# A new slot table for the stages of a chunked delta-rule attention kernel

## What is computed

```
q, k, v = silu(short_conv(x @ W))          # 4 taps along time, 56 tiles of 128 channels
beta = 2 sigmoid(x @ Wb);  g = -exp(A_log) softplus(x @ Wa + dt_bias)
q, k = l2norm(q) / sqrt(d), l2norm(k)
def step(S, t):                            # scan over 1024 tokens, S is 128x128 per head
    S = S * exp(g[t])
    for i in range(3):
        S = S + beta[i] * outer(k[i], v[i] - k[i] @ S)
    return S, q @ S
o = o * rsqrt(mean(o*o) + 1e-5) * rms_weight * silu(x @ Wg)
x = layernorm(x + o @ Wo)
x = layernorm(x + moe(x))
```

## Time and profile before

| | |
|---|---|
| runs | 8394.54, 8353.07, 8391.29 us |
| profiled execution | 8395.38 us, span 8393.3 us |
| granted clock of TensorE, mean | 0.938 |
| TensorE: matmuls, weight loads | 7601.8 us (91%), 6484.1 us (77%) |
| VectorE | 6505.2 us (78%) |
| ScalarE | 5331.5 us (64%) |
| GpSimd | 4114.8 us (49%) |
| moved by DMA | 97.66 MB, 12 GB/s |

### The profile page before, as it was taken

How to read it: one execution, slowest core, us unless ns; L and a number is a source line. 1 busy time by engine, 2 the same in 40 slices (tenths; PEclk the granted TensorE clock), 3 DMA queues, 4 the chain that set the end, 5 groups by cost and what they waited for, 6 DMA issues and landing times. The chain is left out here.

```text
span 8393.3 us, 425998 instructions
## 1 busy us (share of the span) xinstructions
PE 7601.8 (91%) x155940; PEld 6484.1 (77%) x155940; DVE 6505.2 (78%) x22297; ACT 5331.5 (64%) x19575; POOL 4114.8 (49%) x6333
## 2 busy tenths in 40 slices
PE   4799999999999999999999999999999999979999
PEld 1688888888888888888888888888888888857777
DVE  3888888888888888888888888888888888623333
ACT  2666677766766666767666666766776676523333
POOL 0355555555555555555555555555555555511111
PEclk6799999999999999999999999999999999989999
DMA  2000000000000000000000000000000000010000
GB/s 87 6 10 9 10 10 10 10 9 9 10 9 10 9 10 9 10 9 9 10 9 10 9 9 10 9 9 9 10 10 9 9 10 9 8 31 8 10 7 8
DMA packets 283622, 97.66 MB, mean 12 GB/s; under 512 B 226096, under 2 KB 276544, under 8 KB 281152
## 3 DMA queue, kind: packets, MB, share of 16 engines
q1 hardware_dynamic: 281408, 68.93, 3.8%
HBM read 52.08 MB, written 16.78 MB: 8 GB/s over the span
## 5 line engine op out<-in xcount | busy, mean ns | idle before, releaser
L802 DVE SCALAR_TENSOR_TENSOR CY<-PP,CWV,CY 128x128 f32<-128x128 f32 x4608 | 1585.2, 344 | 102.4 <-ACT CY L721 18.0
L802 DVE SCALAR_TENSOR_TENSOR CY<-PP,CWK,CY 128x128 f32<-128x128 f32 x4608 | 1581.9, 343 | 97.6 <-ACT CY L721 26.9
L1014 POOL TENSOR_TENSOR UM<-U,C 32x256 f32<-32x256 f32 x1536 | 1104.7, 719 | 120.2 <-POOL UM L1014 23.1
L1007 POOL TENSOR_TENSOR Y<-U,C 32x256 f32<-32x256 f32 x768 | 554.0, 721 | 1224.1 <-DVE UQ L895 1183.9
L536 PE MATMUL PI<-T,WB 32*32 32x32 f32 x49152 | 750.2, 196 | 302.1 <-DVE T L811 297.3
L536 PEld LDWEIGHTS PI<-T,WB 32*32 32x32 f32 x49152 | 638.4, 110 | 466.8 <-issue 402.4
L516 PE MATMUL PP<-XT,WV 128*128 128x131 f32 x3072 | 741.5, 324 | 157.8 <-DVE CY L802 99.3
L516 PE MATMUL PP<-XT,WK 128*128 128x131 f32 x3072 | 783.5, 340 | 85.0 <-DVE CY L802 84.8
L721 ACT ACTIVATE CY<-PP,CWK 128x128 f32<-128x128 f32 x1536 | 563.1, 367 | 397.9 <-PE PP L516 387.6
L987 POOL TENSOR_TENSOR S<-R,BETA 96x4 f32<-96x4 f32 x512 | 101.3, 198 | 1421.7 <-DVE R L855 1421.7
L791 ACT ACTIVATE KQ<-CY 128x128 f32<-128x128 f32 x2048 | 738.7, 361 | 7.9
(11 more groups left out here) (228 smaller groups left out, 19287.5 us busy)
## 6 DMA issues: line engine op xcount, KB each, us to landing
EX<-exd SPq DMA_DIRECT2D x768, 32.0 KB, 2.2
exd<-EXS SPq DMA_DIRECT2D x16, 512.0 KB, 2.7
XR<-in_L_attn_x SPq DMA_DIRECT2D x65, 64.0 KB, 2.7
XL<-in_L_attn_x SPq DMA_DIRECT2D x16, 256.0 KB, 2.8
XRES<-in_L_attn_x SPq DMA_DIRECT2D x64, 64.0 KB, 2.7
x<-X SPq DMA_DIRECT2D x64, 64.0 KB, 1.6
XI<-x SPq DMA_DIRECT2D x16, 256.0 KB, 2.8
out<-OUT SPq DMA_DIRECT2D x16, 256.0 KB, 2.3
```

Source lines behind the costliest of these rows:

```text
L802: dve.scalar_tensor_tensor(CY[:, m % RING], ptile(m)[:, s:s + P], taps_of(m)[:, s:s + 1], CY[:, m % RING], ALU.mult, ALU.add).then_inc(tap ...
L1007: pool.tensor_tensor(Y1[r, :, :], U[r, par, :, r], over(first[r, :], [BK, NHEAD, BK], 1), ALU.mult).then_inc(seed_sb, 1)
L1014: pool.tensor_tensor(UM[r, lv], U[r, par, :, r], over(merge[lv][r, :], [BK, NHEAD, BK], 1), ALU.mult).then_inc(made, 1)
```

## The change

The stages get new slots. Nothing is computed in another way, and no instruction of the stages is added or taken away.

- Steps of the inversion: at slots 0, 2, 4, 5, 8, 9, 11, 12 instead of 1, 3, 4, 6, 8, 10, 12, 13. Three pairs now stand in adjacent slots. The transposes follow: X2 at slot 6, X3 at 13 (part 0), X1 at 11.
- Second product with the old state at 5 instead of 4, its BZ at 6 instead of 5.
- Gram products at 6 and 7 instead of 7 and 9; U and UQ at 7 and 8 instead of 7 and 9, so one slot behind the product. KD at 5 and 6, SSE and R2 at 3 and 4.
- Output part: squares at 0 and 4, FA at 5, OG at 9 and 10, its transposes and their copies at 12 and 13, the product with Wo at slot 0 of chunk 3, YL at slot 1, layer norm at 4, 5 and 10. Gate products at 7 and 10 instead of 8 and 10.
- GpSimd makes FB and RS after the masks EM of its call, not ahead of them.

The words that came with the change also say that VectorE writes all steps of a level. In the code this is as before: ScalarE copies the first step of each level, now at slots 0 and 8, and VectorE subtracts the other six.

```diff
-INV_AT = {1: 0, 3: 1, 4: 2, 6: 3, 8: 4, 10: 5, 12: 6, 13: 7}
+INV_AT = {0: 0, 2: 1, 4: 2, 5: 3, 8: 4, 9: 5, 11: 6, 12: 7}
...
+                        if k == 0 and norm_now:
+                            pe.wait_ge(ogt_sb, 2 * (i - 1))
+                            for h in range(NHEAD):
+                                mm = pe.matmul(PB[:, 0:P], OGT[:, h], WO[:, h], start=(h == 0), stop=(h == NHEAD - 1))
+                            mm.then_inc(wo_ps, 1)
-                        if k in (1, 4) and do_run:
-                            old_state(k // 4, run, rs, rc)
+                        if k in (1, 5) and do_run:
+                            old_state(k // 5, run, rs, rc)
...
-                        if k in (7, 9) and do_prep:
-                            gram(k // 9, c, sc, prep)
+                        if k in (6, 7) and do_prep:
+                            gram(k - 6, c, sc, prep)
...
-                        if k in (8, 10) and out_now:
-                            l = (k - 8) // 2
+                        if k in (12, 13) and out_now:
+                            l = k - 12
...
-                        if k in (8, 10) and gate_now:
-                            l = (k - 8) // 2
+                        if k in (7, 10) and gate_now:
+                            l = k // 10
...
-                        if k == 12 and out_now:
-                            pe.wait_ge(ogt_sb, 2 * (i - 1))
```

On ScalarE:

```diff
-                        if k in (0, 1) and out_now:
+                        if k in (0, 4) and out_now:
...
-                        if k in (5, 7) and do_prep:
-                            l = k // 7
+                        if k in (5, 6) and do_prep:
+                            l = k - 5
```

On VectorE:

```diff
-                    if do_inv and INV_AT.get(k) == 3 and part == 1:
+                    if do_inv and k == 6 and part == 0:
...
-                    if do_inv and INV_AT.get(k) == 7 and part == 1:
+                    if do_inv and k == 13 and part == 0:
...
-                    if k in (3, 5) and do_prep and part == 0:
+                    if k in (3, 4) and do_prep and part == 0:
...
-                    if k in (2, 5) and do_run:
+                    if k in (2, 6) and do_run:
...
-                    if k == 2 and out_now and part == 0:
+                    if k == 5 and out_now and part == 1:
...
-                    if k in (6, 8) and out_now:
-                        q, l = i - 2, (k - 6) // 2
+                    if k in (9, 10) and out_now:
+                        q, l = i - 2, k - 9
...
-                    if k in (7, 9) and do_prep:
-                        l = k // 9
+                    if k in (7, 8) and do_prep:
+                        l = k - 7
...
-                    if k == 13 and out_now and part == 1:
+                    if k == 1 and norm_now and part == 1:
...
-                    if k == 12 and do_prep and part == 1:
+                    if k == 11 and do_prep and part == 1:
```

More of the change, by code:

```diff
@@ L623, in program @@
                     next_x = c == 3 and known(i + 1, 1, NSC)
+                    norm_now = c == 3 and known(i - 2, 0, NSC)
                     for k in range(SLOTS):
@@ L732, in program @@
                             need(act, wo_ps, i - 2)
-                            for h in heads[k]:
+                            for h in heads[k // 4]:
                                 op = act.activation(OGT[:, h], OSB[:, h // 2, h % 2], ACT.Square, accum_out=SSO[:, h:h + 1])
@@ L762, in program @@
                             act.activation(OSB[:, rc], PA[:, 0:2], ACT.Copy).then_inc(o_sb, 1)
[L763 to L770, removed]
+                        if k in (7, 10) and gate_now:
+                            q, l = i - 1, k // 10
                             act.wait_ge(gate_ps, 2 * q + l + 1)
@@ L781, in program @@
                             op.then_inc(vp_sb, 1)
+                        if k in (12, 13) and out_now:
+                            q, l = i - 2, k - 12
+                            act.wait_ge(ogt_ps, 2 * q + l + 1)
+                            act.wait_ge(sso_sb, 2 * q + 2)
+                            to = OGT[:, :, 2 * CT * l:2 * CT * l + 2 * CT].rearrange("p h (c t) -> p c h t", c=2)
+                            act.activation(to, PB[:, :].rearrange("p (c h t) -> p c h t", c=2, h=NHEAD), ACT.Copy).then_inc(ogt_sb, 1)
                         j, jh, m = lagged(i, half, SLOTS * c + k - 3)
@@ L850, in group @@
                         dve.tensor_scalar(SSE[:, lanes[l]], SSR[:, c, lanes[l]], EPS_L2, None, ALU.add).then_inc(sse_sb, 1)
-                    if k in (3, 5) and do_prep and part == 1:
-                        l = k // 5
+                    if k in (3, 4) and do_prep and part == 1:
+                        l = k - 3
                         dve.wait_ge(sse_sb, 2 * prep + l + 1)
@@ L902, in group @@
                         dve.tensor_tensor(YL[:, :], PB[:, 0:P], XRES[:, half], ALU.add).then_inc(y_sb, 1)
-                    if k == 0 and norm_now and part == 0:
+                    if k == 4 and norm_now and part == 1:
                         dve.wait_ge(y_sb, i - 1)
                         dve.bn_stats(ST[:, :], YL[:, :]).then_inc(st_sb, 1)
-                    if k == 0 and norm_now and part == 1:
+                    if k == 5 and norm_now and part == 0:
                         dve.wait_ge(st_sb, i - 1)
@@ L909, in group @@
                         dve.bn_aggr(MV[:, :], ST[:, :]).then_inc(mv_sb, 1)
-                    if k == 1 and norm_now and part == 0:
+                    if k == 5 and norm_now and part == 1:
                         dve.wait_ge(mv_sb, 2 * (i - 2) + 1)
                         dve.tensor_scalar(MV[:, 1:2], MV[:, 1:2], EPS_LN, None, ALU.add).then_inc(mv_sb, 1)
-                    if k == 4 and norm_now and part == 1:
+                    if k == 10 and norm_now and part == 0:
                         q = i - 2
@@ L974, in program @@
                             pool.wait_ge(diag_sb, NBK * run + b + 1)
[L975 to L982, removed]
                     if do_prep:
```

16 lines of the change are left out of this document (11 added, 5 removed).

## The result

The change made the kernel slower. Four runs of the changed kernel have a median of 8517.99 us (8481.75 to 8538.37), four of the kernel before 8381.37 us (8353.07 to 8394.54): a ratio of 1.0166, 95% interval 1.0127 to 1.0204. The prediction had 8266, range 8120 to 8440. The profiled execution took 8517.22 us.

The account below looks back on a forecast made before the run. No engine is full; VectorE is nearest, waiting mostly for TensorE in a loop between the two. Per block 9.3 us goes and 7.35 comes: 1.95 times 64 is 125 off 8395.4, so 8270, median 8266; range 8120 to 8440.

Parts of the forecast that it names:

- Waits that go: VectorE's waits for Gram product 5.2, subtractions 4.1, scale FA 0.8 us a block; 0.8 stays, so 9.3 goes.
- Plain chunks, 0.28, 1.35 and 0.07: New VectorE waits at inversion steps 5, 6 and 7 in plain chunks: 1.7 us a chunk, 3.4 for two.
- The border to chunk 3, 1.7: Output product ahead of chunk 3's slot 1: VectorE waits 0.5 at YL, 1.2 at step 1's subtraction.
- Gates in chunk 3, 1.25: Gate products at slots 7 and 10 delay VectorE 0.55 at step 5, 0.65 at step 6, 0.05 at step 7.
- ScalarE late in chunk 2, 0.6: ScalarE's squares at slot 4, ahead of the KD rows, come late: between nothing and 1.2 us, taken as 0.6.
- FB and RS at nothing: FB and RS move behind the EM masks on GpSimd, which had been waiting for VectorE anyway: no cost.
- Slots 9 and 10 carry OG, 1.1 us each on VectorE: In chunk 2, OG in these slots takes VectorE 1.1 us each, which covers both waits there.
- The clock: Low-clock stretches of chunks 2 and 3 go, as TensorE's idle time splits into three of about 0.9 us.
- rival 2: Clock falls in plain chunks too (slots 1 to 5), 1.7 us each: 8638, one more only 8529; chance 0.18, shared.
- rival 1: Clock in chunks 2 and 3 stays as it is: 2.4 us a block, 8420, no change; chance 0.20, shared.
- signs that I named: Gram waits under 10, slot 11 waits 1.2 to 1.5, chunk 2 PEclk 1.00; wrong: PEclk under 0.9, VectorE over 90% busy.
- theory A: From the experiments: VectorE instructions whose operands all lie in SBUF are held while GpSimd runs a large product.

Follow-up runs that it names:

- one half alone: The kernel before with its slot table kept and only the output part moved to the changed kernel's places: 8219.27 us, ratio 0.9825.
- the fastest kernel: Kernel before with its old slot table, output part spread as in the change, OG, QSE and X1 moved to slot 8: 8020.33 us, ratio 0.9584.

## Why the prediction was wrong, step by step

- **Waits that go**: right. The Gram wait fell to 6.0 per 1000 us, as forecast (under 10).
- **Plain chunks, 0.28, 1.35 and 0.07**: right in the sum (0.41, 1.03 and 0.22 in the mean of chunk 1, with 0.22 more at a tap). Slots 9, 11 and 12 of a plain chunk:

```profile
3013.05 0.42 DVE L812 TENSOR_TENSOR T<-Y,PI 96x256 f32<-96x256 f32 x1 [0.46 <-PE PI L536]
...
3015.49 0.35 DVE L803 SCALAR_TENSOR_TENSOR CY<-PP,CWK,CY 128x128 f32<-128x128 f32 x1 [0.22 <-ACT CY L722]
3016.88 0.42 DVE L812 TENSOR_TENSOR T<-Y,PI 96x256 f32<-96x256 f32 x1 [1.03 <-PE PI L536]
...
3019.78 0.42 DVE L812 TENSOR_TENSOR Y<-Y,PI 96x256 f32<-96x256 f32 x1 [0.22 <-PE PI L536]
```

  The cause is the one given: TensorE idles 0.71 for ScalarE's copy, and step 6 stands behind the product:

```profile
3015.03 0.97 PEld L591 LDWEIGHTS PK<-BZ,KD 96*128 96x128 f32 x8 [0.71 <-issue]
3016.12 0.59 PEld L536 LDWEIGHTS PI<-T,WB 32*32 32x32 f32 x48
```

  A plain chunk at full clock takes 24.9 to 25.2 us; 24.7 was forecast.
- **The border to chunk 3, 1.7**: 0.2 to 0.4 too much. In this block YL waits 0.17, a tap 0.17, the subtraction at slot 2 1.13; the mean of all blocks is 1.3:

```profile
3055.07 0.29 DVE L903 TENSOR_TENSOR YL<-PB,XRES 128x128 f32<-128x128 f32 x1 [0.17 <-PE PB L633]
...
3057.28 0.42 DVE L812 TENSOR_TENSOR T<-Y,PI 96x256 f32<-96x256 f32 x1 [1.13 <-PE PI L536]
```

- **Gates in chunk 3, 1.25**: 0.44, 0.25 and 0.22 at slots 9, 11 and 12; 0.3 too much.
- **ScalarE late in chunk 2, 0.6**: near nothing. VectorE waits 0.03 us in all in chunk 2 of the changed kernel, and 0.10 with OG in slot 8, where no held product can cover a wait. **FB and RS at nothing**: right for their own time, FB ends over 4 us ahead of the first OG.
- **"Slots 9 and 10 carry OG, 1.1 us each on VectorE": this step failed.** Against the same slots without it (1.36 and 1.16 us in the run with OG in slot 8) OG adds 2.9 and 2.1 us in even blocks, 1.8 and 2.1 in odd ones. That is 2.4 more a block than the 2.1 it adds in slot 8, and about 2.3 more than the prediction's 2.2. I took VectorE's durations from the rows of before as fixed, and asked of GpSimd only whether it would be late, not what it runs beside. "I cost that at nothing" for FA falls under the same error (171 and 166 ns became 414 and 582).
- **The clock**: half right. Low clock went from 11.8 to 7.7 us a block, but only chunks 2 and 3 were relieved, from 9.9 to 2.8. In chunks 0 and 1 it rose from 1.9 to 4.9; of the 122 plain chunks of the loop 8 had a fall of the clock begin in them before and 69 have now, one more in each block, which is a part of rival 2. In the plain chunk with a fall, TensorE idled 0.96 and was then granted 0.50:

```profile
3003.50 0.71 PEld L536 LDWEIGHTS PI<-T,WB 32*32 32x32 f32 x48 [0.96 <-issue]
...
3004.66 1.84 PEld L548 LDWEIGHTS PA<-S,KQ 128*128 128x128 f32 x8
```

```profile
3004.00:3005.00 1.00, 1.00 (x23) 0.94 (x16) 0.87 (x3) 0.22 (x1) 1.00 (x5) 0.50 0.06 16
```

  A chunk with such a fall takes 26.6, 1.7 more, the price I gave to rival 2. Which execution falls stays open: with the same idle times of the weight loads (0.9 and 0.7 us) chunk 1 kept its clock in 21 blocks and lost it in 13. The rule I had set aside (the Trainium skill, "TensorE: Matmul & The Clock Gate", section "A second HAM failure mode: psum-queue depth-cycling": short idles between groups make the clock swing) was the better guide here.

The forecast missed by 252 us, 3.9 a block. The held OG is 2.4 of it (shown by the run in slot 8). Chunks 0 and 1 together lie 2.2 a block above twice 24.9, where I had allowed 0.8: 1.4 more. The rows put nearly all of it down to the clock, since a plain chunk at full clock takes 25.0 in the mean and one with a fall 26.6 to 26.7; no run removes that alone.

Rival 2 with one more fall a block stood at 8529, close to the 8518 measured. That is luck. Its sum held the low clock of chunks 2 and 3 as before (rival 1, 2.4 a block), and that went; the held OG, which no rival had, costs the same 2.4. None of the signs that I named looks at the lengths of VectorE's instructions.

## What to carry to other kernels

Before an instruction of VectorE is moved, look at what GpSimd runs beside its new place, and where its operands lie; its duration in the old trace is only good for the old neighbours. A busy time that changes at an unchanged count of instructions is the sign to look for. Two halves of a change that remove the same wait don't add up in what they gain, while each keeps its cost: run each alone, since here one half alone was 299 us better than the whole.

## What the runs showed of the hardware

OG with two inputs in SBUF takes 343 ns alone, 538 to 875 in the mean beside a product of GpSimd that takes 720. GpSimd gives way less, but it does: UM takes 745 ns in the mean where an OG overlaps it (up to 876) and 721 where none of the lengthened instructions does, a seed 786 (up to 1040) and 721. The Trainium skill, "SBUF — State Buffer", section "Who interferes with whom", states that a VectorE instruction with two SBUF inputs contends with a GpSimd instruction that reads SBUF, and that one with at most one SBUF input outside the two-port modes does not. The traces agree: OG is held, the taps with one input in PSUM stay at 344 ns. The same section of the Trainium skill calls the shared pair of ports an exclusive lock, and says of the two-port modes that whoever issues first gets it for the whole instruction. A hold of that length isn't seen at GpSimd's power operation: 246 OG products beside RT (1.64 us) took 345 ns in the mean in the fastest kernel. Some one-input instructions lose as much: SSE, an addition of a constant on 128x4, takes 159 ns alone and up to 886 beside EM, and X1 346 alone and 826 beside the unit add, while R2 keeps 162; in which mode these ran, no run shows. So theory A's "all operands in SBUF" is too wide: what lengthened here are OG and the second step of FA, with two inputs, and among the one-input instructions SSE, QSE, X1 and the first step of FA.
